# Four-layer attention and expert kernel: early row gathers for the relu layer, reordered loads, early output-projection weights

## What is computed

```
h = layernorm(x);  e = argmax(h @ gate);  s = softmax(h @ gate)[e]
x = x + s * (act(h @ w1[e]) @ w2[e])                  # routed expert layer
q = layernorm(x) @ Wq; k = ctx @ Wk; v = ctx @ Wv     # cross-attention
x = x + (softmax(q k^T + ...) v) @ Wo + bo
```

## Time and profile before

| | us |
|---|---|
| median of 3 runs | 3261.21 (3260.91 to 3267.33) |
| the profiled execution, its time | 3267.9 |
| its span, first to last instruction | 3266.1 |
| PE busy | 2840.0 (87%) |
| DVE busy | 2287.3 (70%) |
| ACT busy | 2054.8 (63%) |
| POOL busy | 1361.2 (42%) |
| mean granted TensorE clock | 0.923 of full |

### The profile page before, as it was taken

The page is one execution under the profiler, slowest core; times in us unless marked ns, Lnnn a source line. Parts: engine busy times, 40 slices in busy tenths (PEclk is TensorE's granted clock), DMA queues, the critical chain, the costliest instruction groups (busy, mean ns, idle before and its releaser), DMA issues. The chain is left out here.

```text
span 3266.1 us, 69990 instructions
## 1 busy us (share of the span) xinstructions
PE 2840.0 (87%) x27595; PEld 1942.1 (59%) x27595; DVE 2287.3 (70%) x3447; ACT 2054.8 (63%) x3053; POOL 1361.2 (42%) x975
## 2 busy tenths in 40 slices
PE   6769998674869999879999778888999999999878
PEld 3236666433436666535666678576666666666777
DVE  6968887668777885578998454767555556557665
ACT  3448888266648887458889322666656566646566
POOL 2249998220128887207888233560000000007433
PEclk8979999796979999889999889887999999999889
DMA  3511111300222221234555465102222222127265
GB/s 115 184 62 56 56 53 41 129 0 26 91 47 56 56 54 27 78 97 109 152 149 152 183 214 197 39 12 73 78 78 78 79 78 78 52 63 215 66 217 192
DMA packets 240761, 308.99 MB, mean 95 GB/s; under 512 B 136135, under 2 KB 182517, under 8 KB 227381
## 3 DMA queue, kind: packets, MB, share of 16 engines
q1 hardware_dynamic: 225659, 250.43, 25.3%
q0 software_dynamic: 12544, 51.65, 4.5%
q10 hardware_dynamic: 2233, 2.39, 0.2%
HBM read 198.45 MB, written 68.62 MB: 82 GB/s over the span
## 5 line engine op out<-in xcount | busy, mean ns | idle before, releaser
L2685 POOL TENSOR_TENSOR lta_p_lo<-lta_p,lta_p_hi 128x1024 f16<-128x1024 f32 x256 | 556.2, 2202 | 178.4 <-DVE lta_p_hi L2808 178.0
L2884 ACT ACTIVATE lta_p<-lta_banks,lw_gmax 128x512 f32<-128x512 f32 x512 | 323.9, 683 | 94.7 <-PE lta_banks L2723 91.3
L2791 DVE TENSOR_REDUCE lta_s_ps<-lta_s_ps 128x1 f32<-128x1101 f32 x240 | 314.1, 1309 | 83.8 <-PE lta_s_ps L2701 83.8
L4808 PE MATMUL m_y_ps<-m_w,m_hT 128*128 128x256 f16 x3072 | 357.4, 273 | 2.1 <-DVE m_hT L4968 2.1
L4796 PE MATMUL m_h_ps<-m_x,m_w 128*128 128x512 f16 x1536 | 353.3, 380 | 3.3 <-issue 3.3
L4893 ACT ACTIVATE m_h<-m_h_ps,m_h_bias,m_h_scale 128x512 f32<-128x512 f32 x256 | 199.4, 779 | 232.7 <-PE m_h_ps L4796 224.5
L4808 PEld LDWEIGHTS m_y_ps<-m_w,m_hT 128*128 128x128 f16 x3072 | 300.0, 98 | 66.0 <-issue 7.9
L4968 DVE TENSOR_TENSOR m_hT<-m_h,m_hT 128x512 f16<-128x512 f32 x256 | 176.2, 692 | 202.0 <-ACT m_hT L4893 198.2
L1234 POOL TENSOR_TENSOR c0a_tri_p_lo<-c0a_tri_p,c0a_tri_p_hi 128x1024 f16<-128x1024 f32 (+2 forms) x192 | 285.7, 1522 | 58.6 <-DVE c0a_tri_p_hi L1408 57.9
L4796 PEld LDWEIGHTS m_h_ps<-m_x,m_w 128*128 128x128 f16 x1536 | 150.5, 98 | 159.9 <-issue 5.9
L1483 ACT ACTIVATE c0a_tri_p<-c0a_banks,c_size 128x512 f32<-128x512 f32 (+3 forms) x384 | 208.4, 577 | 45.4 <-PE c0a_banks L1302 34.1
(11 more groups left out here) (882 smaller groups left out, 6664.7 us busy)
## 6 DMA issues: line engine op xcount, KB each, us to landing
m_w<-rp_w SPq DMA_DIRECT2D x23, 1024.0 KB
m_w<-pw_w SPq DMA_DIRECT2D x23, 1024.0 KB
ltp_pieces<-in_L_ffn_w_dram SPq DMA_DIRECT2D x16, 1024.0 KB, 5.3
lw_room<-in_L_ffn_w_dram SPq DMA_DIRECT2D x16, 1024.0 KB, 7.8
rp_w<-lw_room SPq DMA_DIRECT2D x16, 1024.0 KB, 5.2
m_raw<-in_L_ffn_W_dram SPq DMA_DIRECT2D x16, 1024.0 KB, 7.1
pwo_raw<-in_L_ffn_w_dram POOLq DMA_DIRECT2D x16, 1024.0 KB, 8.7
pw_w<-pwo_pair POOLq DMA_DIRECT2D x16, 1024.0 KB, 4.4
```

What stands on the lines that cost most here:

```text
L2685: nc.gpsimd.tensor_tensor(p_lo[:, slot, :], p32[:, p32_slot(h, j), :], p_hi[:, slot, :], ALU.subtract).then_inc(rested, 1)
L2791: nc.vector.tensor_reduce(ntop_of(h)[:, n:n + 1], scores(h, n), AX_X, ALU.max, negate=True).then_inc(top_ready, 1)
L2884: nc.scalar.activation(p32[0:rows, slot, c * 512:(c + 1) * 512], t_ps[0:rows, c, :], ACT.Exp, bias=bias, scale=p["gmax"][0:rows, 0:1]).the ...
L4808: last = nc.tensor.matmul(y_ps[:, q, 0:D], hT[:, k % 2, a, f, q * P:(q + 1) * P], w2[:, v, b, f, :], start=f == 0 and m == 0, stop=f == FC ...
```

## The change

- In `route_rows`, POOL no longer returns early for the relu layer: it waits for the stored rows (one store more than in layer 3, the zero row) and for `ids`, and issues the first `EARLY_FETCHES` = 4 gathers. The relu stage issues gathers 4 to 6 when it opens. The gathered rows lie in `room[:, 0:4]`, a buffer of the latent stage, and the relu stage now runs inside the scope that holds it, so the clearing block of that scope comes behind the relu stage and no longer ahead of it.
- In `cross_operands` with `combine` (layer 2), the order of loads is x group 0, Wk, Wv, x groups 1 to 3, Wq, and the rest as before.
- `Projection` is a new class with its own `Stage` (two semaphores) and the buffers `wo` and `bo`. In layers 2 and 3 its load is issued in `cross_operands`, behind the mask and the three side loads and ahead of the 9 MB. In layer 0 the load stays where it was.

```diff
+EARLY_FETCHES = 4
+
+def fetched_rows(room):
+    return room[:, 0:4, :].rearrange("p a n -> p (a n)")[:, 0:XS_RING * ROW].rearrange("p (k n) -> p k n", k=XS_RING)
...
-        if pairs is None:
-            return
-        pool.wait_ge(r["x_stored"], 16 * (TILES // 4))
+        pool.wait_ge(r["x_stored"], 16 * (TILES // 4) + (16 if pairs is None else 0))
         pool.wait_ge(r["rows_stored"], 16 * (TILES // 4))
         pool.wait_ge(ids_ready, 1)
-        for j in range(XS_RING):
+        for j in range(EARLY_FETCHES if pairs is None else XS_RING):
             gather_rows(nc, pool, r, j)
...
-            for j in range(XS_RING):
+            for j in range(EARLY_FETCHES, XS_RING):
                 gather_rows(nc, pool, r, j)
...
-        if combine is not None:
-            for g in range(groups):
+        def load_x(some):
+            for g in some:
...
+        if combine is not None:
+            load_x(range(0, 1))
         sp.dma_start(wk[:], mat("Wk")).then_inc(wk_loaded, 16)
         sp.dma_start(wv[:], mat("Wv")).then_inc(wv_loaded, 16)
+        if combine is not None:
+            load_x(range(1, groups))
         sp.dma_start(wq[:], mat("Wq")).then_inc(wq_loaded, 16)
...
         if bias is not None:
             for g in range(Side.RING):
                 bias.load(sp, g)
+        projection.load(sp)
         if routed is not None:
             routed.load_expansion(sp)
...
+class Projection:
+    def __init__(self, nc, ctx, tag, weight, bias):
+        st = Stage(nc, ctx, tag + "w")
+        self.weight, self.bias = weight, bias
+        self.wo, self.bo = st.sb("wo", [P, DC, D]), st.sb("bo", [P, D])
+        self.loaded, self.bias_loaded = st.sem("loaded"), st.sem("bias_loaded")
+    def load(self, sp):
+        sp.dma_start(self.bo[:], self.bias.partition_broadcast(P)).then_inc(self.bias_loaded, 16)
+        sp.dma_start(self.wo[:], self.weight.rearrange("(c p) n -> p c n", p=P)).then_inc(self.loaded, 16)
...
-        sp.dma_start(bo[:], bias.partition_broadcast(P)).then_inc(bias_loaded, 16)
-        sp.dma_start(wo[:], weight.rearrange("(c p) n -> p c n", p=P)).then_inc(loaded, 16)
...
-        relu_experts_stage(nc, env, "m1", routed)
+            relu_experts_stage(nc, env, "m1", latent.room, routed)
```

More of the change, by code:

```diff
@@ L215, in _, with add_projection_stage @@
                         gate(t)
-def add_projection_stage(nc, env, tag, rows, weight, bias, beside=None):
+def add_projection_stage(nc, env, tag, rows, projection, beside=None):
     with ExitStack() as ctx:
@@ L226, in add_projection_stage @@
             beside.open(ctx)
-        wo, bo = st.sb("wo", [P, DC, D]), st.sb("bo", [P, D])
+        early = isinstance(projection, Projection)
+        if not early:
+            projection = Projection(nc, ctx, tag, *projection)
+        wo, bo, loaded, bias_loaded = projection.wo, projection.bo, projection.loaded, projection.bias_loaded
         rT = st.sb("rT", [P, RING, DC, P])
         t_ps, y_ps = st.ps("t_ps", [P, T_RING, 512]), st.ps("y_ps", [P, RING, 512])
-        loaded, bias_loaded, turned, evacuated, y_done, biased, added, summed = (
-            st.sem(n) for n in ("loaded", "bias_loaded", "turned", "evacuated", "y_done", "biased", "added", "summed"))
+        turned, evacuated, y_done, biased, added, summed = (
+            st.sem(n) for n in ("turned", "evacuated", "y_done", "biased", "added", "summed"))
         block = ctx.enter_context(nc.Block())
@@ L3393, with projected_routed_stage @@
 XS_RING, W2_RING = 7, 3
-def projected_routed_stage(nc, env, tag, name, args, rows, weight, bias, func, pairs, out):
+def projected_routed_stage(nc, env, tag, name, args, rows, projection, func, pairs, out):
     w = lambda n: args[f"{name}_{n}"]
@@ L3418, in projected_routed_stage @@
         with nc.Block() as block:
-            project_rows(nc, env, Stage(nc, ctx, tag + "p"), block, w, weight, bias, r)
+            project_rows(nc, env, Stage(nc, ctx, tag + "p"), block, w, projection, r)
             route_rows(nc, env, Stage(nc, ctx, tag + "r"), block, w, None,
@@ L3434, in project_rows @@
     lg_ps, lg_done = banks[:, 6, :], r["lg_done"]
-    loaded, bias_loaded, gate_loaded, turned, evacuated, y_done, biased, added, summed = (
-        st.sem(n) for n in ("loaded", "bias_loaded", "gate_loaded", "turned", "evacuated", "y_done", "biased", "added", "summed"))
+    gate_loaded, turned, evacuated, y_done, biased, added, summed = (
+        st.sem(n) for n in ("gate_loaded", "turned", "evacuated", "y_done", "biased", "added", "summed"))
     linked, var_ready, std_ready, normed, x_turned, x_evac = (
@@ L4156, in cross_attention_stage @@
         st = Stage(nc, ctx, tag)
+        if projection is None:
+            projection = Projection(nc, ctx, tag, w("Wo"), w("bo"))
         qT, kbd = st.sb("qT", [P, DC, T]), st.sb("kbd", [P, DC, B, H // DC * NCTX])
@@ L4161, in cross_attention_stage @@
         with ExitStack() as inner:
-            cross_operands(nc, env, Stage(nc, inner, tag + "p"), inner, w, mask, hides, qT, kbd, v16, v_back, neg, bias, combine, routed)
+            cross_operands(nc, env, Stage(nc, inner, tag + "p"), inner, w, mask, hides, qT, kbd, v16, v_back, neg, bias, combine, routed,
+                           projection)
         out = st.sb("out", [P, TILES, D]) if into is None else into
```

33 lines of the change are left out of this document (17 added, 16 removed).

## The result

The changed kernel takes 3256.32 us, the median of 10 runs (3250.1 to 3258.97), beside 3265.09 for the kernel before in 10 runs (3260.91 to 3270.33). The ratio is 0.9969, interval 0.9961 to 0.9977, which is 10.1 us less (7.5 to 12.7). The forecast was 15.8 us less and 3245.4 us. So the direction held, the time lies above the range, and 5.7 us of gain are missing. The rest of the 10.9 us between 3245.4 and 3256.32 is no error in the reasoning on the change: 3.9 us because the three runs that I started from had a median of 3261.21 and the ten have 3265.09, and 1.3 us because the two medians lie 8.8 us apart where the ratio gives 10.1.

The account below looks back on a forecast made before the run. PE, busy 87% of the span, was taken as the bound, so only its waits at stage starts could give time. 7.3 + 3.7 + 2.8 + 3.3 - 1.35 = 15.75 us off 3261.21 gave 3245.4, range 3240.0 to 3252.5.

Parts of the forecast that it names:

- Relu layer: From routing's end to the first expansion: four gathers issued early let the expansion start sooner, gain 7.3 us.
- The block closes 0.3 us later than now: End of the routing program: POOL finishes issuing gathers at 1888.5, 0.3 us after DVE, delaying the close by that much.
- my first rival: Routing's end: POOL's program cannot close until its gathers land; gain falls to 1.9 us, time 3250.9; chance 0.10.
- the 4.3 us of my lower bound: Routing's end: DVE work holds all four early gathers by 0.74 us each, leaving 4.3 us of gain.
- Layer 2's operands: Wk loaded directly behind x group 0 lets the second group's queries start 3.7 us earlier; bounds 0 and 4.9.
- Layer 2's projection: PE's idle 2.81 us for `wo` go: gain 2.8 us, bounds 2.4 and 3.8.
- my bound of 3.8: Upper bound in layer 2's projection: PE may reach full clock one tile sooner, gain 3.8 us.
- Layer 3's projection: PE's wait for `wo` goes and POOL's bias adds start earlier, freeing DVE's merge: gain 3.3 us, bounds 2.2 and 3.4.
- the limit that I had named: Layer 3's projection: the gain is limited by the end of POOL's bias adds, at 3.4 us.
- The side tile: Layer 3: early `bo` and `wo` loads could delay the fourth side tile; taken as 0, bound 1.0 us.
- Clearing blocks: Layer 0's projection, behind layer 2's attention, and kernel's end: one more block each, together costing 1.35 us.
- The clock rival: Layer 2's gated experts: tighter stages get a lower TensorE clock; at 3.5% the time is 3267; chance 0.03.

Follow-up runs that it names:

- The two repeats: The changed kernel executed again, unedited, two single executions for further profiles: 3257.06 and 3257.14 us.

## Why the prediction was wrong

- **Relu layer, 7.3 forecast, 4.7 to 4.9 measured.** The step that failed: "The block closes 0.3 us later than now", because POOL "is done at 1888.5". POOL's instructions are done there, its program is not. It closes when the gathers have landed. That was my first rival, and I gave it 0.10 on the ground that no row showed it and nothing in the program asks for it. The drains of 3.8 and 2.7 us in the profile before did show that POOL's ends are not free; I looked only at the clearing blocks behind them. My last paragraph named the sign, a drain of several us at the end of routing, and it came. The gain that the rival left, 1.9 us, was too small: it took 6.7 us from issue to landing from a row beside the `w2` loads, and with no loads beside it the fourth gather landed 4.1 us after its start (1883.43 to 1887.48). With 4.1 in its place the rival gives 1891.3 for the landing and 4.5 us of gain, an estimate that comes near the 4.7 to 4.9. A smaller slip beside it: I called the 4.30 us of the first expansion a time at half clock. The clock had risen 3.0 us into it; at half throughout it took 5.28.
- **What might have slowed the gathers did not.** They took 1.55, 0.96, 0.95 and 0.95 us beside the routing's DVE steps, so the 4.3 us of my lower bound came near by another cause. Beside DVE's copies of weights, in the relu stage, one took 1.86 us. The Trainium skill, page SBUF — State Buffer, section "SBUF: two separate sides", says that a DVE copy in its two-port mode keeps GpSimd from writing descriptors; the trace agrees for the copies, and no effect of it shows in the stretch on which the sum rests.
- **Layer 2's operands, 3.7 forecast.** Right in mechanism and in one profile (3.5, with `bq` as the next hold). In two others of the same kernel 3 us of it go to the clock, of which the attention gives back 1.1: operands and attention together gain 3.5, 1.6 and 1.2 us. My sum held every duration at the level that one profile happened to show.
- **Layer 2's projection, 2.8 forecast, 3.2, 4.0 and 4.0 measured** up to the clearing steps behind it. The two repeats lie above my bound of 3.8, and by what that bound was made of: the clock rose sooner.
- **Layer 3's projection, 3.3 forecast, 0.2 to 1.5 measured.** The head start was there, 3.4 us. The step that failed is that it was carried to the end of the stage; the granted clock was back at half sooner, and the products at the stage's end ran at twice their length. The merge on DVE was held by POOL no shorter than before, 1.38 us beside 1.23; that it ends 3.4 us earlier is the limit that I had named. This agrees with the rule of the Trainium skill that I had cited from the page SBUF — State Buffer, section "Who interferes with whom"; what I had wrong is that the hold would go: the adds and the merge both began earlier, and the merge was again held until POOL's last add, over two of the adds.
- **The side tile, 0 forecast with a bound of 1.0: 1.0 measured.** The term was put at nothing because no wait stood in the list, but that said nothing on how much slack there was. The wait of 1.1 to 1.2 us in the three profiles is gone with the load put back.
- **Clearing blocks, 1.35 forecast, 1.2 measured** in the first profile: 0.22 us at the end of the kernel (2.86 from the drain's end became 3.08), 0.68 behind layer 2's attention, 0.33 in layer 0's projection. Small beside the rest.
- **The clock rival.** I looked for it in layer 2's experts, where it did not appear (719.0 to 719.6 us beside 720.2). It appeared in two short stages whose waits the change took out, in some executions. What makes the level fall there stays open.

By stretches the forecast was too high by 2.4 to 2.6 us in the relu layer, 0.2 to 2.5 in layer 2's operands and attention together, 1.8 to 3.1 in layer 3's projection and 1.0 for the side tile, and too low by 0.4 to 1.2 in layer 2's projection. Over all that lies behind the last routing step the forecast was 16.2 us (15.75 and the block of 0.45 in layer 0), and the three profiles gained 10.8, 11.4 and 10.2: 5.4, 4.8 and 6.0 are missing, beside 5.7 by the ratio, with 2.6 to either side. The named stretches would make more; part of it came back where nothing was forecast, 0.6 to 1.2 us of it in layer 2's experts, for which no run gives a reason.

## What to carry to other kernels

Where POOL issues DMAs, it is done with a program only when its drain is, so before such work is moved to the end of a program, read the drains in POOL's queue and not only its last instruction; of two, three and four early gathers the fewest did best here. Where POOL has issued many DMAs, drain it once where it idles anyway. And in stages as short as the two here (40 and 55 us), price what a removed wait brings at both levels of the clock, and look at several profiles before one of them is believed to 1 us.

## What the runs showed of the hardware

- With everything landed, POOL's drain takes 0.082 us for each DMA that it issued since the last drain, plus 0.05: 0.221 us for 2 to 3.820 us for 46, ten sizes. One with nothing issued and no work left takes 0.034 us. It also ends no sooner than the landings (0.13, 0.17 and 0.21 us behind them for 2, 3 and 4 gathers). SP's drain waits for no landing: 0.129 us, 4.4 us before its last load landed.
- The fourth early gather of 128 rows landed 4.1 us after its start with only the other gathers in flight (3.7 to 4.0 in the seven other profiles with four early), against 6.7 for a gather beside the weight loads.
- The same kernel, executed again, gets its clock falls in other places: layer 2's operands took 37.23, 40.17 and 40.62 us, layer 3's projection 55.76, 54.59 and 54.54.
